# du earlier on GpSimd, its transposes and copies one slot earlier, delta replicated with 16 transfers

## The chip, the cores and the metric

The program runs on one core of a Trainium2 chip. The metric is the device time of one execution in microseconds, the median of several runs. A core has five engines that run their own instruction streams and meet only at semaphores: TensorE (PE in the profile, its weight loads PEld), VectorE (DVE), ScalarE (ACT), GpSimd (POOL) and the SyncE queue (SP), which here only issues DMA transfers.

## The reference

A Mamba network of four layers over 16 sequences of 256 tokens with 128 features, then a layer norm, a mixture of experts (8 experts, the best 2 of each token) and a second layer norm, all in float32. The part that the change touches is one layer:

```python
xp, z = split(rmsnorm(x) @ Win)
xc = silu(conv4(xp) + conv_b)
dt, B, C = split(xc @ Wx)
delta = softplus(dt @ Wdt + bdt)
for t in range(T):            # per channel d (256) and state n (16)
    h = exp(delta[t] * A) * h + (delta[t] * xc[t]) * B[t]
    y[t] = sum_n(h * C[t])
x = x + ((y + xc * D) * silu(z)) @ Wblk
```

`delta * xc` is called du in the kernel, exp(delta*A) decay, du*B dbu.

## The kernel before

Tokens go in 8 groups of 512 (two sequences), layers in 4, so there are 32 steps (`STEPS`). A step has 16 slots (`SLOTS`): slot 4m+p scans for state block m (0 to 3) and the pair p of channel units 2p and 2p+1. A unit is 32 channels times 4 states on the 128 partitions. For every slot VectorE runs one scan (L799) over 1024 columns and, for even slots, the product by C (L808, issued after the next scan). GpSimd makes the product by C of the odd slots (`times_c`, L466). TensorE adds the products up over the states (`quad`, L1000) into y.

What a scan needs is made by three engines. ScalarE makes decay with two exponentials per slot (`exps`, L545) from `d_rep`, in which delta stands four times, once for each group of 32 partitions. `outer` makes dbu with time on the partitions, from the transposed du (`du_t`) and a column of B: for each m there are 16 products, eight on GpSimd (L457 and L460) and eight on ScalarE (L623). TensorE turns them back (`to_channels`, L1015, eight transposes per slot) into `dbu_ps`, which has two buffers, so the transposes of slot n wait for scan n-2. Only at the first pair of each m do they also wait for all 16 products.

The order on each engine is written out by hand, as code under `if slot == ...` in five functions named `window(s, i, par)`. The window of step s holds the scans of step s and everything that prepares step s+1: convolution and projections, softplus (ScalarE at slots 7 and 8, VectorE after scan 8, where L838 gives `delta_ready`), du on GpSimd (L484), du's eight transposes on TensorE (`turn_du`, L1093), their two copies on ScalarE (`copy_dut`, L608), and the products of m = 0. The `SHARE`, `FIRST`, `POOL_SHARE` and `POOL_FIRST` tuples at the top say how many of the products are issued at which slot. The steps are unrolled but for the middle ones, which are a loop over pairs of windows (`par` 0 and 1).

`replicate` (L351) issues the copies of delta into `d_rep`: for each of 8 units and 4 partition groups one transfer of 32 partitions by 512 elements, 64 KB. Four semaphores per buffer (`rep_ready`) count them, one for each pair p; the exponentials of m = 0 wait for their pair's.

## Time and profile before

| | |
|---|---|
| median of 3 runs | 2284.54 us (2284.45 to 2295.04) |
| profiled execution | 2288.18 us, its span 2286.4 us |
| mean granted TensorE clock | 0.923 |
| busy in the span | VectorE 1951.5 us (85%), TensorE 1921.3 (84%), ScalarE 1687.4 (74%), GpSimd 1508.2 (66%) |
| first scan, last scan start | 67.0 us, 1823.6 us |

The span is from the first to the last instruction. About 1755 us of it is the 32 steps, the rest is the start and the experts at the end. A time in a timeline row is counted from the start of the span, so the same instruction can be compared across engines; a bracket at a row's end gives how long the engine stood idle before the row, and what it waited for. A busy share is a mean over stages and says nothing of which wait ended last.

### The profile page before, as it was taken

To read this page: it belongs to the slowest core of one execution; us is meant where nothing else is said; L and a number is where in the kernel's file an instruction comes from. 1 tells how busy PE (TensorE), PEld (TensorE's weight loads), DVE (VectorE), ACT (ScalarE), POOL (GpSimd) and SP (SyncE) were. 2 spreads that over 40 slices of the span, in tenths; PEclk is the share of its full clock that TensorE was granted. 3 is DMA by queue.
4 is the path that set the end of the run, shared out by engine and by line. 5 is a ranking of instruction groups with operands and counts; after the bars stand their busy time and mean duration, and the time that the engine had idled before them with its cause. 6 is when DMAs were issued, how large, how long until landed. Compare 5 with 4: busy or idle time off the path is not lost.

```text
span 2286.4 us, 35098 instructions
## 1 busy us (share of the span) xinstructions
PE 1921.3 (84%) x10784; PEld 1205.6 (53%) x10784; DVE 1951.5 (85%) x1824; ACT 1687.4 (74%) x3050; POOL 1508.2 (66%) x1365
## 2 busy tenths in 40 slices
PE   4688888888888888888888788888887689999998
PEld 1444444444444444444444444444444368998998
DVE  3799898998999998998999999998999976776776
ACT  3888888888888888888888888888888423333333
POOL 2688888888888888888888888888888700000000
PEclk8899998999999999999999999998999889999999
DMA  7323222222222323232323223222322200000000
GB/s 233 80 66 74 66 73 58 73 58 73 58 73 58 74 59 75 60 76 59 75 61 77 75 66 76 65 76 60 76 62 66 92 1 10 10 11 10 9 6 10
DMA packets 81482, 139.49 MB, mean 61 GB/s; under 512 B 21264, under 2 KB 39312, under 8 KB 76816
## 3 DMA queue, kind: packets, MB, share of 16 engines
q1 hardware_dynamic: 75024, 120.36, 20.5%
q10 hardware_dynamic: 6400, 18.42, 3.3%
q8 instruction: 30, 0.49, 0.1%
q14 instruction: 28, 0.23, 0.0%
HBM read 63.85 MB, written 7.74 MB: 31 GB/s over the span
## 4 chain that ended last, share of the span: by engine, by line
PE 34%; ACT 23%; POOL 17%; issue 11%; DVE 7%; ACTq 1%; POOLq 0%; DVEq 0%
PE y_ps L1215 10%; ACT decay L545 9%; POOL scan L466 8%; PE dbu_ps L1191 8%; POOL scan L460 8%; PE dbu_ps L1015 6%; PE pre_ps L1028 5%; ACT scan L623 5%; DVE scan L799 5%; PE pre_ps L1038 2%; POOL scan L457 2%; ACT sp_e L582 1%; ACT delta L583 1%; PE y_ps L1000 1%; ACT sp_l L592 1%
## 5 line engine op out<-in xcount | busy, mean ns | idle before, releaser
L799 DVE TENSOR_TENSOR_SCAN scan<-decay,dbu_ps 128x1024 f32<-128x1024 f32 x512 | 1157.3, 2276 | 151.4 <-PE dbu_ps L1015 147.1
L466 POOL TENSOR_TENSOR scan<-scan,c_rep 128x1024 f32<-128x1024 f32 x256 | 722.8, 2823 | 263.3 <-DVE scan L799 190.0
L1015 PE MATMUL dbu_ps<-ident,scan 128*128 128x128 f32 x4096 | 605.3, 296 | 287.3 <-DVE scan L799 181.9
L1015 PEld LDWEIGHTS dbu_ps<-ident,scan 128*128 128x128 f32 x4096 | 505.3, 152 | 619.7 <-DVE scan L799 303.8
L545 ACT ACTIVATE decay<-d_rep,a_cur 128x510 f32<-128x510 f32 x1024 | 670.7, 710 | 138.3 <-DMA d_rep<-delta 82.5
L460 POOL TENSOR_SCALAR scan<-du_t,b_t 128x256 f32<-128x256 f32 x896 | 591.5, 677 | 0.0
L623 ACT ACTIVATE scan<-du_t,b_t 128x256 f32<-128x256 f32 x1024 | 442.5, 494 | 1.2
L808 DVE TENSOR_TENSOR scan<-scan,c_rep 128x1024 f32<-128x1024 f32 x256 | 328.0, 1281 | 0.0
L1000 PE MATMUL y_ps<-scan,sel 128*32 128x512 f32 x2048 | 300.5, 661 | 5.7 <-POOL scan L466 5.7
L737 ACT ACTIVATE decay<-dbu_ps 128x512 f32<-128x512 f32 x256 | 148.6, 598 | 209.8 <-PE dbu_ps L1191 198.7
L1028 PE MATMUL pre_ps<-xn,w_pre 128*128 128x512 f32 x512 | 274.5, 663 | 5.7 <-DVE w_pre L788 4.9
L495 POOL TENSOR_TENSOR sp_e<-sp_e,bout_rep 128x512 f32<-128x512 f32 x8 | 10.9, 1361 | 295.9 <-DMA sp_e<-in_x_rows 295.9
L955 DVE TENSOR_TENSOR decay<-decay 128x512 f32<-128x512 f32 x256 | 164.5, 687 | 22.9 <-ACT decay L737 21.8
L1191 PE MATMUL dbu_ps<-y_parts,w_hi 128*128 128x512 f32 x512 | 166.3, 406 | 6.3 <-issue 5.6
L1028 PEld LDWEIGHTS pre_ps<-xn,w_pre 128*128 128x128 f32 x512 | 100.0, 217 | 110.9 <-issue 104.4
L942 DVE SCALAR_TENSOR_TENSOR xc<-y_ps,cw,xc 128x128 f32<-128x128 f32 x256 | 72.1, 344 | 100.5 <-PE y_ps L1215 100.5
L1215 PEld LDWEIGHTS y_ps<-w_pre,decay 128*128 128x128 f32 x1024 | 120.7, 194 | 5.5 <-issue 3.0
L1215 PE MATMUL y_ps<-w_pre,decay 128*128 128x128 f32 x1024 | 121.2, 277 | 2.5 <-DVE decay L955 2.5
L1215 PEld LDWEIGHTS y_ps<-c_rep,decay 128*128 128x128 f32 x1024 | 118.5, 192 | 2.0
L1215 PE MATMUL y_ps<-c_rep,decay 128*128 128x128 f32 x1024 | 118.5, 275 | 0.0
L1191 PEld LDWEIGHTS dbu_ps<-y_parts,w_hi 128*128 128x128 f32 x512 | 93.8, 192 | 24.7 <-issue 6.1
L1191 PE MATMUL dbu_ps<-y_parts,w_lo 128*128 128x512 f32 x256 | 101.5, 397 | 0.0
(105 smaller groups left out, 1737.7 us busy)
## 6 DMA issues: line engine op xcount, KB each, us to landing
d_rep<-delta SPq DMA_DIRECT2D x1024, 64.0 KB, 2.0
c_rep<-c_rows SPq DMA_DIRECT2D x32, 1024.0 KB
w_pre<-prepared_weights ACTq DMA_DIRECT2D x15, 866.0 KB, 10.4
prepared_weights<-scan SPq DMA_DIRECT2D x3, 1122.0 KB, 23.9
scan<-in_conv_w SPq DMA_DIRECT2D x4, 512.0 KB, 4.6
w_out<-prepared_weights SPq DMA_DIRECT2D x16, 128.0 KB, 9.8
sp_e<-in_x_rows SPq DMA_DIRECT2D x8, 256.0 KB, 3.3
d_rep<-in_w ACTq DMA_DIRECT2D x2, 1024.0 KB, 7.5
```

Of the source, the lines that this page charges most:

```text
L460: nc.gpsimd.tensor_scalar(dst, src, col, 1.0, ALU.mult, ALU.mult).then_inc(dbut_pool, 1)
L466: nc.gpsimd.tensor_tensor(ring[slot % RING], ring[slot % RING], c_rep[par][:, slot // PRS, :].unsqueeze(1).broadcast_to([128, 2, TG]), ALU ...
L545: last = nc.scalar.activation(decay[slot % DEC][:, u, :, 1:], src[:, :, 1:], ACT.Exp, scale=a_cur[:, b, m:m + 1])
L623: nc.scalar.activation(dbu_t[m % 2][:, j, :, q, :], du_t[par][:, j, :].rearrange("p (b c) -> p b c", b=UNITS), ACT.Copy, scale=b_t[par][:, ...
L799: nc.vector.tensor_tensor_scan(ring[slot % RING].rearrange("p u t -> p (u t)"), decay[slot % DEC].rearrange("p u a t -> p (u a t)"), dbu_p ...
L808: nc.vector.tensor_tensor(ring[slot % RING], ring[slot % RING], c_rep[par][:, slot // PRS, :].unsqueeze(1).broadcast_to([128, 2, TG]), ALU ...
L955: nc.vector.tensor_tensor(hid[e % 2][:, c, :], hid[e % 2][:, c, :], hid[e % 2][:, c, :], ALU.mult).then_inc(h2_ready, 1)
L1000: last = nc.tensor.matmul(y_ps[k][CH * j:CH * j + CH, :], sel[:, :], ring[slot % RING][:, j % 2, :], start=False, stop=m == M - 1, skip_gr ...
L1015: last = nc.tensor.transpose(dbu_ps[slot % 2][:, u, 128 * j:128 * j + 128], dbu_t[m % 2][:, j, b, :, :].rearrange("p q c -> p (q c)"), ide ...
L1028: tap = nc.tensor.matmul(o, w_pre[:, c0:c0 + 128], xn[:, :, k:k + SEQ], start=k == 0, stop=k == KC - 1, skip_group_check=True)
L1191: last = nc.tensor.matmul(dst, left[l], right[r], start=start and n == 0, stop=stop and n == len(passes) - 1)
L1215: last = nc.tensor.matmul(moe_ps[e % 2][:, DM * j:DM * j + DM], hid[e % 2][:, c, 128 * j:128 * j + 128], w2_sb[e][:, c, :], start=c == 0, ...
```

## The change

The diff makes four edits:

1. GpSimd issues du at the start of slot 10, before the last two products of m = 3 and the product by C of slot 9 that stand in that slot. It was behind them.
2. TensorE issues du's transposes at the end of slot 11, not of slot 12. ScalarE's copy of the previous group's output out of the same PSUM bank (`copy_out`, L630), which the transposes wait for, goes from slot 12 to slot 11.
3. ScalarE issues du's two copies at slot 14, not 15, and its eight products of m = 0 as 3, 3 and 2 at slots 14, 15 and 0, where it had 3 and 5 at slots 15 and 0.
4. `replicate` issues 16 transfers of 128 KB: one brings row group r of both halves k, that is units r and r+4. Two semaphores count them. Pairs 0 and 2 wait for the first eight transfers, pairs 1 and 3 for the last eight.

`POOL_FIRST` becomes (0, 0, 2, 3, 4): GpSimd's products of m = 0 are dealt out otherwise over slots 13 and 14, between which no other GpSimd instruction stands.

```diff
--- before.py
+++ after.py
@@ -46,9 +46,9 @@
 POOL_OUTER = Q * POOL_J
 ACT_OUTER = Q * (JT - POOL_J)
 SHARE = (0, 2, 5, 8)
-FIRST = (0, 3, 8)
+FIRST = (0, 3, 6, 8)
 POOL_SHARE = (0, 2, 3, 4, 4)
-POOL_FIRST = (0, 0, 1, 3, 4)
+POOL_FIRST = (0, 0, 2, 3, 4)
 
 
 W_CONV = 0
@@ -224,7 +224,7 @@
         dbut_pool = sem("dbut_pool")
         dbut_act = sem("dbut_act")
         dbu_ready = sem("dbu_ready")
-        rep_ready = [[sem(f"rep_ready{i}_{p}") for p in range(PRS)] for i in range(2)]
+        rep_ready = [[sem(f"rep_ready{i}_{p}") for p in range(2)] for i in range(2)]
         a_cur_ready = sem("a_cur_ready")
         decay_ready = sem("decay_ready")
         scan_done = sem("scan_done")
@@ -345,11 +345,11 @@
 
                 wait(sp, decay_ready, SLOTS * (s - 1))
                 sp.wait_ge(delta_ready, s + 1)
-                for b in range(UNITS):
-                    k, row = b // Q, CH * (b % Q)
+                by_row = d_rep[par].rearrange("p (k r) t -> p r k t", k=KT)
+                for r in range(Q):
                     for q in range(Q):
-                        sp.dma_start(d_rep[par][CH * q:CH * q + CH, b, :], delta[row:row + CH, k, :])\
-                            .then_inc(rep_ready[par][b // 2], 16)
+                        sp.dma_start(by_row[CH * q:CH * q + CH, r, :, :], delta[CH * r:CH * r + CH, :, :])\
+                            .then_inc(rep_ready[par][r // 2], 16)
 
             def load_input(g, n, par):
 
@@ -471,6 +471,10 @@
                 nxt = 1 - par
                 for slot in range(SLOTS):
                     m = slot // PRS + 1
+                    if slot == 10 and has(s, 1):
+                        pool.wait_ge(delta_ready, s + 2)
+                        nc.gpsimd.tensor_tensor(du[:, :, :], delta[:, :, :], xc[nxt][:, :, :], ALU.mult)\
+                            .then_inc(du_ready, 1)
                     if m < M and has(s, 0):
                         outer(s, par, m, POOL_SHARE[slot % PRS], POOL_SHARE[slot % PRS + 1])
                     if m == M and has(s, 1):
@@ -479,10 +483,6 @@
                         times_c(s - 1, i if par else i - 1, nxt, SLOTS - 1)
                     elif slot % 2 == 0 and slot and has(s, 0):
                         times_c(s, i, par, slot - 1)
-                    if slot == 10 and has(s, 1):
-                        pool.wait_ge(delta_ready, s + 2)
-                        nc.gpsimd.tensor_tensor(du[:, :, :], delta[:, :, :], xc[nxt][:, :, :], ALU.mult)\
-                            .then_inc(du_ready, 1)
                     if slot == 7 and has(s, 2):
                         normalise(s + 2)
                     if slot == 4 and is_last(s):
@@ -537,7 +537,7 @@
             def exps(s, i, par, slot):
                 m, p = slot // PRS, slot % PRS
                 if m == 0:
-                    act.wait_ge(rep_ready[par][p], 2 * Q * 16 * (i + 1))
+                    act.wait_ge(rep_ready[par][p % 2], 2 * Q * 16 * (i + 1))
                 wait(act, scan_done, SLOTS * s + slot - DEC + 1)
                 for u in range(2):
                     b = 2 * p + u
@@ -656,7 +656,7 @@
                         exps(s, i, par, slot)
                     m, p = slot // PRS + 1, slot % PRS
                     if has(s, 0) and slot == 0:
-                        outer(s, par, 0, FIRST[1], FIRST[2])
+                        outer(s, par, 0, FIRST[2], FIRST[3])
                     if has(s, 0) and m < M and p:
                         outer(s, par, m, SHARE[p - 1], SHARE[p])
                     if slot == 0 and has(s, 2):
@@ -678,14 +678,15 @@
                             load_w_pre(i)
                     if slot == 10 and has(s, 1):
                         copy_bt(s + 1, nxt)
-                    if slot == 12 and has(s, -1):
+                    if slot == 11 and has(s, -1):
                         copy_out(s - 1)
                     if slot == 12 and par == 1 and has(s, 0) and has(s, 1):
                         act.wait_ge(skip_done, s + 1)
                         load_w_skip(i)
-                    if slot == 15 and has(s, 1):
+                    if slot == 14 and has(s, 1):
                         copy_dut(s + 1, nxt)
-                        outer(s + 1, nxt, 0, FIRST[0], FIRST[1])
+                    if slot >= 14 and has(s, 1):
+                        outer(s + 1, nxt, 0, FIRST[slot - 14], FIRST[slot - 13])
                     if is_last(s):
                         if slot == 4:
                             copy_x(0)
@@ -1132,7 +1133,7 @@
                         turn_b(s + 1)
                     if slot == 9 and has(s, -1):
                         project_out(s - 1, i if par else i - 1, nxt)
-                    if slot == 12 and has(s, 1):
+                    if slot == 11 and has(s, 1):
                         turn_du(s + 1)
                     if slot >= 14 and has(s, 2):
                         if par == 0:
```

GpSimd, slots 8 to 13 of one window, as a difference (`-` before, `+` the change). L466 is the product by C, L457 and L460 the products that make dbu, L484 and L476 du:

```order
 L466 TENSOR_TENSOR scan<-scan,c_rep 128x1024 [waits scan_done]
-L460 TENSOR_SCALAR scan<-du_t,b_t 128x8x32 x4
+L460 TENSOR_SCALAR scan<-du_t,b_t 128x8x32 x2
+L476 TENSOR_TENSOR sp_l<-delta,xc 128x1024 [waits delta_ready]
+L460 TENSOR_SCALAR scan<-du_t,b_t 128x8x32 x2
 L466 TENSOR_TENSOR scan<-scan,c_rep 128x1024 [waits scan_done]
-L484 TENSOR_TENSOR sp_l<-delta,xc 128x1024 [waits delta_ready]
 L466 TENSOR_TENSOR scan<-scan,c_rep 128x1024 [waits bt_ready,scan_done,dut_ready,dbu_ready]
 L457 TENSOR_TENSOR scan<-du_t,b_t 128x8x32 [waits bt_ready,dut_ready,dbu_ready]
```

du moved ahead of two products of m = 3 and of the product by C of slot 9; the next product by C (slot 11) stands behind the wait for du's copies (`dut_ready`) as it did.

TensorE, slots 11 to 13, before. L1015 are `to_channels`, L1000 a `quad`, L1093 du's transposes:

```order
L1015 MATMUL dbu_ps<-ident,scan 128x128 [waits scan_done]
L1015 MATMUL dbu_ps<-ident,scan 128x128 x7
L1000 MATMUL y_ps<-scan,sel 32x512 [waits hc_pool,hc_dve]
L1000 MATMUL y_ps<-scan,sel 32x512 x3
L1015 MATMUL dbu_ps<-ident,scan 128x128 [waits scan_done,dbut_act,dbut_pool]
L1015 MATMUL dbu_ps<-ident,scan 128x128 x7
L1093 MATMUL pre_ps<-ident,sp_l 128x128 [waits x_ready,bt_ready,du_ready]
L1093 MATMUL pre_ps<-ident,sp_l 128x128 x7
```

and the same place in the change, where every line number is one higher:

```order
L1016 MATMUL dbu_ps<-ident,scan 128x128 [waits scan_done]
L1016 MATMUL dbu_ps<-ident,scan 128x128 x7
L1001 MATMUL y_ps<-scan,sel 32x512 [waits hc_pool,hc_dve]
L1001 MATMUL y_ps<-scan,sel 32x512 x3
L1094 MATMUL pre_ps<-ident,sp_l 128x128 [waits x_ready,bt_ready,du_ready]
L1094 MATMUL pre_ps<-ident,sp_l 128x128 x7
L1016 MATMUL dbu_ps<-ident,scan 128x128 [waits scan_done,dbut_act,dbut_pool]
L1016 MATMUL dbu_ps<-ident,scan 128x128 x7
```

du's transposes moved ahead of the eight transposes for scan 12.

ScalarE, from slot 14 of one window to slot 0 of the next, as a difference. L545 are exponentials, L608 du's copies, L623 products of m = 0:

```order
-L545 ACTIVATE decay<-d_rep,a_cur 128x2x255 [waits scan_done]
-L545 ACTIVATE decay<-d_rep,a_cur 128x2x255
 L608 ACTIVATE du_t<-pre_ps 128x512 [waits dut_mm] x2
 L623 ACTIVATE scan<-du_t,b_t 128x8x32 [waits bt_ready,dut_ready,dbu_ready]
 L623 ACTIVATE scan<-du_t,b_t 128x8x32 x2
+L545 ACTIVATE decay<-d_rep,a_cur 128x2x255 [waits scan_done]
+L545 ACTIVATE decay<-d_rep,a_cur 128x2x255
+L623 ACTIVATE scan<-du_t,b_t 128x8x32 x3
 L545 ACTIVATE decay<-d_rep,a_cur 128x2x255 [waits scan_done,rep_ready1_0]
 L545 ACTIVATE decay<-d_rep,a_cur 128x2x255
-L623 ACTIVATE scan<-du_t,b_t 128x8x32 x5
+L623 ACTIVATE scan<-du_t,b_t 128x8x32 x2
```

The copies and the first three products passed the exponentials of slot 15, and three of the five products left for slot 0 did too.

## Rows read from the trace of the kernel before

**Rows 1.** The waits of VectorE from 112 to 1735 us: total, times, longest.

```profile
DVE scan L799 <- PE dbu_ps L1015: 116.0, 90, 2.6
```

**Rows 2.** Busy time by engine in one step, from its first scan to the next's.

```profile
949.34:1005.34 56.00, 47.23 (x245) 25.74 (x244) 50.16 (x29) 47.67 (x87) 47.50 (x44) 0.90 0.32 75
```

**Rows 3.** VectorE's timeline: start, duration, instruction, idle before it and its releaser.

```profile
984.66 1.19 DVE L808 TENSOR_TENSOR scan<-scan,c_rep 128x1024 f32<-128x1024 f32 x1
990.16 1.33 DVE L808 TENSOR_TENSOR scan<-scan,c_rep 128x1024 f32<-128x1024 f32 x1
...
1001.50 1.26 DVE L808 TENSOR_TENSOR scan<-scan,c_rep 128x1024 f32<-128x1024 f32 x1
1005.34 2.29 DVE L799 TENSOR_TENSOR_SCAN scan<-decay,dbu_ps 128x1024 f32<-128x1024 f32 x1 [2.58 <-PE dbu_ps L1015]
1008.57 2.29 DVE L799 TENSOR_TENSOR_SCAN scan<-decay,dbu_ps 128x1024 f32<-128x1024 f32 x1 [0.94 <-PE dbu_ps L1015]
1012.39 2.29 DVE L799 TENSOR_TENSOR_SCAN scan<-decay,dbu_ps 128x1024 f32<-128x1024 f32 x1 [0.42 <-PE dbu_ps L1015]
```

**Rows 4.** TensorE's timeline in the same step.

```profile
986.70 1.93 PE L1000 MATMUL y_ps<-scan,sel 128*32 128x512 f32 x8
988.56 1.52 PE L1015 MATMUL dbu_ps<-ident,scan 128*128 128x128 f32 x8
990.53 1.09 PE L1093 MATMUL pre_ps<-ident,sp_l 128*128 128x128 f32 x8 [0.45 <-POOL sp_l L484]
...
998.35 1.99 PE L1028 MATMUL pre_ps<-xn,w_pre 128*128 128x512 f32 x4
1003.24 1.96 PE L1015 MATMUL dbu_ps<-ident,scan 128*128 128x128 f32 x8 [2.91 <-POOL scan L460]
```

**Rows 5.** TensorE at another boundary between two steps.

```profile
283.92 1.09 PE L1015 MATMUL dbu_ps<-ident,scan 128*128 128x128 f32 x8 [2.91 <-POOL scan L460]
```

**Rows 6.** VectorE at that other boundary.

```profile
287.64 2.29 DVE L799 TENSOR_TENSOR_SCAN scan<-decay,dbu_ps 128x1024 f32<-128x1024 f32 x1 [0.20 <-PE dbu_ps L1015]
```

**Rows 7.** GpSimd's timeline in the step of rows 3 and 4.

```profile
978.13 4.76 POOL L460 TENSOR_SCALAR scan<-du_t,b_t 128x256 f32<-128x256 f32 x4
984.83 3.26 POOL L466 TENSOR_TENSOR scan<-scan,c_rep 128x1024 f32<-128x1024 f32 x1 [1.94 <-DVE scan L799]
988.04 2.36 POOL L484 TENSOR_TENSOR sp_l<-delta,xc 128x1024 f32<-128x1024 f32 x1
...
992.73 2.38 POOL L466 TENSOR_TENSOR scan<-scan,c_rep 128x1024 f32<-128x1024 f32 x1 [2.33 <-ACT du_t L608]
...
995.65 3.26 POOL L460 TENSOR_SCALAR scan<-du_t,b_t 128x256 f32<-128x256 f32 x5
...
1001.21 1.90 POOL L460 TENSOR_SCALAR scan<-du_t,b_t 128x256 f32<-128x256 f32 x2
```

**Rows 8.** ScalarE's timeline in that step, and once at the start of the program.

```profile
61.53 1.33 ACT L545 ACTIVATE decay<-d_rep,a_cur 128x510 f32<-128x510 f32 x2 [13.31 <-DMA d_rep<-delta]
...
987.74 3.86 ACT L545 ACTIVATE decay<-d_rep,a_cur 128x510 f32<-128x510 f32 x6
991.51 1.06 ACT L608 ACTIVATE du_t<-pre_ps 128x512 f32<-128x512 f32 x2
...
1004.59 1.33 ACT L545 ACTIVATE decay<-d_rep,a_cur 128x510 f32<-128x510 f32 x2 [2.46 <-DMA d_rep<-delta]
```

**Rows 9.** SyncE's transfers of delta in that step: start and time to issue all.

```profile
982.63 20.51 SPq L351 DMA_DIRECT2D d_rep<-delta  x32
```

**Rows 10.** The page's costliest groups, ScalarE's products: busy, mean ns, idle before.

```profile
L623 ACT ACTIVATE scan<-du_t,b_t 128x256 f32<-128x256 f32 x1024 | 442.5, 494 | 1.2
```

**Rows 11.** Issue of the output transfers (256 KB each): ns min/median/max.

```profile
L408 SPq DMA_DIRECT2D out<-delta x8: 377/389/400, 1913.8 to 2283.6; - x8
```

**Rows 12.** Busy by engine, clock, DMA share and GB/s in two stretches.

```profile
990.00:1003.10 13.10, 9.63 (x57) 5.15 (x56) 12.77 (x8) 12.11 (x25) 10.78 (x12) 1.00 0.44 105
...
1003.24:1005.20 1.96, 1.96 (x9) 1.96 (x10) 0.00 (x0) 0.61 (x1) 1.96 (x5) 0.50 0.25 59
```

## The prediction

> **What bounds the kernel now.** I read the waits of each engine first, from the second step to the 31st. VectorE is the engine that the steps run on: in one step of 56.00 us it is busy 50.16 us [rows 2], more than any other. Almost all that it lacks is one wait: scans for TensorE's transposes, 116.0 us in 90 waits [rows 1]. VectorE's timeline shows where they are: three per boundary between two steps, at scans 0, 1 and 2 (30 boundaries in that stretch), 2.58, 0.94 and 0.42 us in the step that I work with [rows 3], 116.0 / 30 = 3.87 us at a boundary in the mean. From there one goes back by the releasers. TensorE's transposes for scan 0 start at 1003.24, although TensorE was done with its work before at 998.35 + 1.99 = 1000.34; they waited for GpSimd's last product of m = 0 [rows 4], which ended at 1001.21 + 1.90 = 1003.11 [rows 7]. GpSimd had stood still for 2.33 us before 992.73, for ScalarE's copies of du [rows 7]. These came at 991.51 to 992.57, behind six exponentials [rows 8], and du's transposes had been done only at 991.62, having waited 0.45 us for du [rows 4], which GpSimd made at 988.04 to 990.40, 5.4 us after delta was ready: SyncE's copies of delta, which wait for the same semaphore, start at 982.63 [rows 7, 9]. So the chain is delta, du, transposes, copies, GpSimd's products, transposes, scan 0. The change shortens just this chain.
>
> **The chain, step by step**, in the times of that step.
>
> *du.* It starts at 982.6, like SyncE's copies, and takes 2.36 us [rows 7]: 985.0, 5.4 us earlier. Before it GpSimd has done two of the four products that begin at 978.13, by about 980.5, and then waits 2.1 us for delta with the other two queued behind it. Nobody misses them: they end at about 987, and their reader is the transpose block for scan 12, which began at 988.56 before [rows 4]. The product by C of slot 9 follows, 987 to 989.4; before it ended at 988.1. It is read by a `quad` at slot 13, after 991.
>
> *Transposes.* They follow the `quad` that ends at 986.70 + 1.93 = 988.63. Eight transposes took 1.52 us there [rows 4], so they end at 990.1, 1.5 us earlier. Now the block for scan 12 stands behind them, and ends at 990.1 + 1.1 = 991.2; VectorE wants it at 990.16 + 1.33 = 991.49 [rows 3]. That is a margin of 0.3 us. With both blocks at the slow length of 1.96 us [rows 4] it would be missed by 1.1 us. I charge 0.15 us.
>
> *Copies.* `copy_out` and the exponentials of slot 12 only change places, so ScalarE comes to slot 13 at 987.74 as before. The six exponentials from there are those of slots 13 to 15, 3.86 us [rows 8]; now only four stand ahead of the copies: 987.74 + 2.57 = 990.3. `copy_out` is done in front of them, in time for the transposes at 988.6. The copies, 1.06 us, end at 991.4, where they ended at 992.57: 1.1 us earlier. It is the exponentials that set them now, not the transposes (990.1). Behind the copies stand eight products of m = 0 at 0.49 [rows 10] and the exponentials of slots 15 and 0 at 1.3 a slot, to about 998; scan 15 wants its decay at 999, scan 0 at 1002.8.
>
> *GpSimd's products.* From 992.73 to 1003.11 GpSimd is busy without a gap, 10.38 us, so its end moves with its start, by 1.1 us. It gains something on top: the last two products take 1.90 us, against 0.65 us each in the five before them [rows 7], beside VectorE's product by C at 1001.50 [rows 3]; when they are over before that begins they take 0.9. End: 991.5 + 10.4 - 0.9 = 1001.0, bounds 1000.5 to 1002.0.
>
> *Scan 0 and scan 1.* TensorE, free at 1000.34, starts its block at 1001.2 after 0.8 us of idleness, not 2.9. The granted clock in this block was 0.50, half of full speed, that is the 1.2 GHz level, while it was 1.00 (2.4 GHz) in the 13 us before [rows 12], and the block took 1.96 us. At another boundary, after the same idleness, it took 1.09 us [rows 5]. With 0.8 us of idleness I take the short one: 1002.3. VectorE comes free at 1001.50 + 1.26 = 1002.76. The wait of 2.58 us is gone. At the boundary with the short block scan 1 waited only 0.20 us [rows 6], with VectorE starting as early as TensorE allowed; now it starts 0.4 us later than that, so this wait is gone too. What is late next is TensorE's row of blocks before scan 2: of the 0.42 us I leave 0.3. Scans 3 to 15 keep their distances.
>
> *The 16 transfers.* 32 issues take 20.51 us, 0.64 each, until 1003.14 [rows 9]. ScalarE waited for the last one until 1004.59, at the exponentials of slot 3 [rows 8], so it lands 1.5 to 2 us after its issue. In the shortened step that would be too late, so the edit matters. The trace has no transfer of this form (32 partitions by 2 by 512). If the price is per issue, 16 take 10.3 us, and all has landed at 995. If it is per byte, 20.5 us. The nearest rows: an output transfer of four times the size, cut in the same way along the free axis, has an issue of 0.39 us [rows 11], and while these copies run alone the DMA engines are busy 0.44 at 105 GB/s [rows 12], so twice the rate would be 0.88: they can just follow. I take 0.65 us each, end 995.1, perhaps 997 where weights are loaded beside it. The exponentials of slot 1 now need all 16 transfers, and come at about 998.
>
> *Start.* The first step waited 13.31 us for its first eight transfers behind stores of weights [rows 8]. Eight now carry twice the bytes: 512 KB more. Between -1 and +5 us, once; I take +2.
>
> **A rule weighed.** VectorE's product by C took 1.19 us at 984.66 and 1.33 us at 990.16, when du was in its last 0.24 us; GpSimd's product by C took 3.26 us when it began together with one of VectorE's and 2.38 otherwise [rows 3, 7]. So the two hold each other up. du now runs over 984.66 to 985.0, and VectorE's product there may be held up by 0.3 us; at 990.16 it no longer is. I charge 0.2 us of VectorE per step for this and for changed meetings elsewhere. The Trainium skill (SBUF — State Buffer, "Who interferes with whom") says that a VectorE instruction with two SBUF inputs and a GpSimd instruction that reads SBUF exclude each other, and that the later one is blocked until the other is through. Taken in full, a VectorE product that comes just after a GpSimd product by C began would lose all its 2.4 us, against the 0.14 us that is seen at 990.16.
>
> **Sum.** 3.87 - 0.3 (left at scan 2) - 0.15 (scan 12) - 0.2 (held up) - 0.17 (boundaries with the long block in one of six, 1 us each) = 3.05 us at a boundary. Times 31 boundaries: 94.5. Less 2 at the start: 92.5. From the profiled execution, 2288.18, that leaves 2195.7. The median of the runs is 3.64 us below it, so I predict 2192.
>
> **Rivals.**
>
> A, transfers priced by byte: slower than before. At 1.28 us each the last lands at 1005.1. Before, slot 1 needed only half of the transfers; now its exponentials stand until 1005.1, and behind them on ScalarE the rest of slots 1 to 3 (three pairs of exponentials and eight products, some 7.5 us), then `silus`, at 1012.6. Before, these followed the exponentials at 1004.59 and three products [rows 8, 10], at 1007.4. Of the 5.2 us ScalarE makes up a part, where it waits for TensorE after that: between 0 and 5.2 us are lost per step, and I take 2.3: 31 x 2.3 = +71, 2356. It decides from 16 transfers that take over 0.88 us each (loss of part of the gain) and 1.14 us each (loss of all). For it: an untried form, and the low DMA reserve. Against it: [rows 11, 12].
>
> B, half the gain: TensorE's block for scan 0 stays long. It ends at 1003.2, scan 0 waits 0.4 us, and scan 1 waits 0.9 as in [rows 3], scan 2 0.4. 3.87 - 1.7 - 0.35 = 1.8 per boundary: -56 + 2, 2231. For it: the long block is the usual one before. Against it: the idleness ahead of it goes from 2.9 to 0.8 us.
>
> C, GpSimd in VectorE's way. With m = 0 done at 1001.1 GpSimd goes straight into four products (2.4 us, and 0.9 held up at 1001.5) and its product by C of slot 15, about 1004.4 to 1006.8; VectorE's next product by C comes after scans 0 and 1, at 1002.8 + 4.5 = 1007.3. If GpSimd is 0.6 us later, VectorE comes while it runs and is held up by about 2 us: 3.05 - 2 = 1.05 per boundary, 2254. This is where the skill's rule would bring it in full.
>
> D, no gain: a wait on the chain that I did not see (du's transposes kept by something else) leaves the copies where they are: 2284.
>
> **Chances.** Forecast 0.65 (own range 2176 to 2214), B 0.14, C 0.08, D 0.05, A 0.08. A change under 0.5%, 11 us, is about what a measurement of this kernel can't tell from none. Faster: 0.65 + 0.14 + 0.08 = 0.87, same 0.05, slower 0.08. Range: from 2175 (3.6 us gained at each boundary) to 2256, which takes in B and C.
>
> **What would show it.** Right: the waits of scans for transposes fall from 116 us to 10 or 20, the step is about 52.1 us; du begins within 0.2 us of delta; copies about 1.1 us earlier in the step; TensorE's idleness before the block for scan 0 under 1 us and the block at 1.1 us; the 16 transfers issued in 10 to 11 us and no wait of ScalarE for `d_rep` but at the start. Wrong: transfers that take over 0.9 us each with ScalarE waiting at slot 1 (A); a long block at clock 0.5 (B); VectorE's products by C above 2 us (C); copies of du no earlier (D).

## The result, and the profile after

| | before | changed |
|---|---|---|
| median | 2284.49 us (2278.19 to 2295.04, 4 runs) | 2177.46 us (2173.84 to 2182.44, 4 runs) |
| ratio to before | | 0.9529, 95% interval 0.9487 to 0.957 |
| profiled execution, its span | 2288.18, 2286.4 us | 2175.6, 2173.8 us |
| mean granted TensorE clock | 0.923 | 0.942 |

The change makes the kernel 4.7% faster, 107 us between the medians and 112.6 us between the profiled executions. 2192 us was forecast, with 2175 to 2256 as the range: right, and 14.5 us too cautious. One execution of e1 (2778.65 us) and one of e7b (3671.61 us), both experiments further down, lie far outside all others of their kernels and are in no median or ratio here.

First VectorE's waits, from the second step to the 31st, in the changed kernel (total, times, longest):

```profile
DVE sp_w L831 <- ACT sp_l L592: 21.1, 29, 0.8
DVE scan L800 <- PE dbu_ps L1016: 7.4, 15, 1.1
DVE scan L800 <- ACT decay L545: 3.8, 11, 0.4
```

The scans waited 116.0 us in 90 waits for TensorE [rows 1] and now 7.4 us in 15. Nothing of that size has come in its place. One step of the changed kernel, from its first scan to the next's (length, then busy of TensorE, weight loads, VectorE, ScalarE, GpSimd, then clock, DMA share, GB/s):

```profile
945.46:997.09 51.63, 44.76 (x247) 24.15 (x246) 50.33 (x31) 48.58 (x89) 46.04 (x44) 0.97 0.28 64
```

VectorE does the same work, 50.33 us against 50.16, in 51.63 us in place of 56.00 [rows 2]. It is now busy 97% of the step. The chain itself, in the changed kernel's timelines of this step. VectorE makes delta, and then waits neither for scans 0 and 1 (997.09) nor for scan 2 (1002.74):

```profile
975.54 1.23 DVE L839 TENSOR_TENSOR delta<-delta,sp_l 128x1024 f32<-128x1024 f32 x1
...
995.76 1.41 DVE L809 TENSOR_TENSOR scan<-scan,c_rep 128x1024 f32<-128x1024 f32 x1
997.09 4.45 DVE L800 TENSOR_TENSOR_SCAN scan<-decay,dbu_ps 128x1024 f32<-128x1024 f32 x2
...
1002.74 2.29 DVE L800 TENSOR_TENSOR_SCAN scan<-decay,dbu_ps 128x1024 f32<-128x1024 f32 x1
```

SyncE's transfers and GpSimd's du, both right behind delta:

```profile
976.84 10.24 SPq L351 DMA_DIRECT2D d_rep<-delta  x16
```

```profile
976.85 2.35 POOL L476 TENSOR_TENSOR sp_l<-delta,xc 128x1024 f32<-128x1024 f32 x1 [2.42 <-DVE delta L839]
...
985.06 2.93 POOL L466 TENSOR_TENSOR scan<-scan,c_rep 128x1024 f32<-128x1024 f32 x1 [1.64 <-ACT du_t L608]
...
994.11 0.94 POOL L460 TENSOR_SCALAR scan<-du_t,b_t 128x256 f32<-128x256 f32 x2
```

TensorE, with du's transposes (L1094) and the block for scan 0 at 995.19:

```profile
982.59 1.09 PE L1094 MATMUL pre_ps<-ident,sp_l 128*128 128x128 f32 x8
...
995.19 1.09 PE L1016 MATMUL dbu_ps<-ident,scan 128*128 128x128 f32 x8 [0.56 <-POOL scan L460]
```

ScalarE, six exponentials and then du's two copies:

```profile
980.17 3.78 ACT L545 ACTIVATE decay<-d_rep,a_cur 128x510 f32<-128x510 f32 x6
983.84 1.06 ACT L608 ACTIVATE du_t<-pre_ps 128x512 f32<-128x512 f32 x2
```

delta ends at 976.77. du begins 0.08 us behind it, the copies end 8.1 us behind it, GpSimd's last product of m = 0 ends at 995.05, and TensorE's block comes after 0.56 us of idleness, not 2.91, and is short. It is over at 996.28, before VectorE is free.

The same reading for all 31 boundaries between two steps gives the table that the experiments are compared by. Its numbers are means made from the timelines, in us. A step is the mean of the 30 from the second step's scan 0 to the 32nd's; the next two columns count from the end of delta. A block (the eight transposes for scan 0) is called long when it takes over 1.5 us.

| kernel | step | copies begin, end | block for scan 0 begins | long blocks |
|---|---|---|---|---|
| before | 55.17 | 8.97, 10.04 | 20.71 | 21 of 31 |
| changed | 51.38 | 7.47, 8.59 | 18.52 | 0 of 31 |
| e1 | 54.99 | 8.96, 10.02 | 20.68 | 20 of 31 |
| e2 | 52.26 | 7.47, 8.58 | 18.53 | 0 of 31 |
| e3 | 55.69 | 9.17, 10.23 | 21.00 | 30 of 31 |
| e4 | 53.26 | 8.96, 10.21 | 20.17 | 1 of 31 |
| e5 | 55.53 | 9.17, 10.23 | 20.98 | 29 of 31 |
| e6 | 51.62 | 7.83, 8.92 | 18.79 | 1 of 31 |
| e8 | 54.61 | 8.76, 9.84 | 20.53 | 23 of 31 |

3.79 us per step, 31 times, is 117.5 us; the profiled executions differ by 112.6. The rest went the other way at the start. VectorE's first scan is at 69.1 and not 67.0, and scan 3 waits 3.87 us and not 1.48, so that the softplus of the second step stands 4.8 us later. What ScalarE waited for, and SyncE's transfers there, in the changed kernel:

```profile
41.57 21.98 SPq L351 DMA_DIRECT2D d_rep<-delta  x16
...
64.76 1.33 ACT L545 ACTIVATE decay<-d_rep,a_cur 128x510 f32<-128x510 f32 x2 [15.55 <-DMA d_rep<-delta]
```

13.31 us of waiting [rows 8] have become 15.55.

### The profile page after: what moved, and what is told of

It reads as the page before. It is cut to its first block, busy times and chain, and to the rows that moved or that the text cites. A ratio compares the mean times of both kernels' runs of the same rounds, so it can differ in the third digit from the quotient of the medians.

```text
span 2173.8 us, 34586 instructions
## 1 busy us (share of the span) xinstructions
PE 1875.8 (86%) x10784; PEld 1179.1 (54%) x10784; DVE 1943.6 (89%) x1824; ACT 1682.6 (77%) x3050; POOL 1460.3 (67%) x1365
## 4 chain that ended last, share of the span: by engine, by line
ACT 29%; POOL 26%; PE 25%; issue 12%; DVE 5%; SPq 1%; DMA 1%; ACTq 1%; POOLq 0%; DVEq 0%
POOL scan L466 12%; ACT decay L545 11%; POOL scan L460 11%; PE y_ps L1216 11%; PE dbu_ps L1192 8%; ACT scan L623 7%; DVE scan L800 3%; POOL scan L457 2%; ACT sp_e L582 2%; ACT delta L583 2%; ACT sp_l L592 2%; PE dbu_ps L1016 2%; ACT sp_e L587 1%; SPq L351 1%; ACT du_t L608 1%
## 5 line engine op out<-in xcount | busy, mean ns | idle before, releaser
L1016 PE MATMUL dbu_ps<-ident,scan 128*128 128x128 f32 x4096 | 570.4, 286 | 236.4 <-DVE scan L800 198.8
L466 POOL TENSOR_TENSOR scan<-scan,c_rep 128x1024 f32<-128x1024 f32 x256 | 676.3, 2642 | 140.8 <-DVE scan L800 75.8
L1016 PEld LDWEIGHTS dbu_ps<-ident,scan 128*128 128x128 f32 x4096 | 479.8, 146 | 516.6 <-DVE scan L800 266.6
L545 ACT ACTIVATE decay<-d_rep,a_cur 128x510 f32<-128x510 f32 x1024 | 668.1, 709 | 72.0 <-DMA d_rep<-delta 29.6
L460 POOL TENSOR_SCALAR scan<-du_t,b_t 128x256 f32<-128x256 f32 x896 | 592.7, 677 | 0.0
L623 ACT ACTIVATE scan<-du_t,b_t 128x256 f32<-128x256 f32 x1024 | 445.6, 494 | 1.2
L809 DVE TENSOR_TENSOR scan<-scan,c_rep 128x1024 f32<-128x1024 f32 x256 | 330.8, 1292 | 0.0
L1029 PE MATMUL pre_ps<-xn,w_pre 128*128 128x512 f32 x512 | 248.4, 608 | 5.6 <-DVE w_pre L789 4.8
L1029 PEld LDWEIGHTS pre_ps<-xn,w_pre 128*128 128x128 f32 x512 | 88.9, 193 | 99.1 <-issue 92.7
L476 POOL TENSOR_TENSOR sp_l<-delta,xc 128x1024 f32<-128x1024 f32 x32 | 75.2, 2350 | 83.7 <-DVE delta L839 83.7
## 6 DMA issues: line engine op xcount, KB each, us to landing
w_pre<-prepared_weights ACTq DMA_DIRECT2D x15, 866.0 KB, 13.8
```

The costliest lines, as they stand in the source:

```text
L460: nc.gpsimd.tensor_scalar(dst, src, col, 1.0, ALU.mult, ALU.mult).then_inc(dbut_pool, 1)
L466: nc.gpsimd.tensor_tensor(ring[slot % RING], ring[slot % RING], c_rep[par][:, slot // PRS, :].unsqueeze(1).broadcast_to([128, 2, TG]), ALU ...
L545: last = nc.scalar.activation(decay[slot % DEC][:, u, :, 1:], src[:, :, 1:], ACT.Exp, scale=a_cur[:, b, m:m + 1])
L623: nc.scalar.activation(dbu_t[m % 2][:, j, :, q, :], du_t[par][:, j, :].rearrange("p (b c) -> p b c", b=UNITS), ACT.Copy, scale=b_t[par][:, ...
L809: nc.vector.tensor_tensor(ring[slot % RING], ring[slot % RING], c_rep[par][:, slot // PRS, :].unsqueeze(1).broadcast_to([128, 2, TG]), ALU ...
L1016: last = nc.tensor.transpose(dbu_ps[slot % 2][:, u, 128 * j:128 * j + 128], dbu_t[m % 2][:, j, b, :, :].rearrange("p q c -> p (q c)"), ide ...
```

## The experiments

**The transfers by themselves.** e1 is the kernel before with edit 4 alone, e2 the changed kernel without it.

```diff
-                for b in range(UNITS):
-                    k, row = b // Q, CH * (b % Q)
+                by_row = d_rep[par].rearrange("p (k r) t -> p r k t", k=KT)
+                for r in range(Q):
                     for q in range(Q):
...
-                    act.wait_ge(rep_ready[par][p], 2 * Q * 16 * (i + 1))
+                    act.wait_ge(rep_ready[par][p % 2], 2 * Q * 16 * (i + 1))
```

e1:

> The kernel before with the 16 transfers alone. Theory (the transfers shorten nothing while the chain delta, du, transposes, copies, GpSimd's products sets the boundary): the waits of scans for transposes stay near 116 us from the second step to the 31st, the waits of ScalarE for d_rep go, and only the start costs something, +4.8 us as after: 2284.5 + 4.8 = 2289, between 2280 and 2292. Rival (ScalarE's waits for d_rep, 67 us in 35 waits, were on the path): about 2220 to 2250.

e2:

> The changed kernel with the 32 transfers of before. Theory: the last of them lands 22 us after delta, ScalarE comes to the exponentials of slot 3 at 19.3 us after delta, waits 2.7 us there, and the projection of z is 1.1 us late in each step (0.5 to 1.6): 2177.5 + 31 x 1.1 - 4.8 (the start as before) = 2207, between 2188 and 2225. Rival (the transfers are hidden in the changed kernel too): 2173, only the start is better. Second rival (all of the gain hangs on them): 2280.

e1: 2290.68 us, ratio 1.0019 (0.9993 to 1.0045), no change. e2: 2200.1 us, ratio 0.9627 (0.9579 to 0.9675), about 1% behind the changed kernel. ScalarE's wait for delta's transfers between 112 and 1735 us, first in the kernel before (there that is the second step to the 31st):

```profile
ACT decay L545 <- DMA d_rep<-delta: 67.1, 35, 2.5
```

then in e2:

```profile
ACT decay L545 <- DMA d_rep<-delta: 74.7, 37, 3.9
```

and VectorE's in e1 and in e2:

```profile
DVE scan L799 <- PE dbu_ps L1015: 111.5, 90, 2.6
```

```profile
DVE scan L800 <- PE dbu_ps L1016: 27.1, 60, 3.5
```

In e1 the 16 transfers cut ScalarE's 67 us of waiting to 14 us and VectorE waits nearly as before: those waits were hidden. In the shortened step the late last transfer is felt, as argued, at 0.88 us per step (52.26 and not 51.38). So edit 4 is worth nothing alone and about 1% beside the others.

**The copies.** e5 is the changed kernel with ScalarE's order of before (copies at slot 15, products 3 and 5). e8 is the reverse, the kernel before with that order alone changed.

```diff
-FIRST = (0, 3, 6, 8)
+FIRST = (0, 3, 8)
...
-                    if slot == 14 and has(s, 1):
-                        copy_dut(s + 1, nxt)
-                    if slot >= 14 and has(s, 1):
-                        outer(s + 1, nxt, 0, FIRST[slot - 14], FIRST[slot - 13])
+                    if slot == 15 and has(s, 1):
+                        copy_dut(s + 1, nxt)
+                        outer(s + 1, nxt, 0, FIRST[0], FIRST[1])
```

e5:

> The changed kernel with ScalarE's two copies of du at slot 15 again, behind all exponentials, and its products of m = 0 as 3 at slot 15 and 5 at slot 0; du and the transposes stay early, the transfers are 16. Theory (the place of the copies sets GpSimd's start): the copies end 10.0 us after delta as before, not 8.1, GpSimd's last product of m = 0 ends near 20.3 us after delta, the waits at scans 0 and 1 come back nearly whole: 2270 to 2289, say 2280. Rival (du and its transposes made the gain): under 2200.

e8:

> The kernel before with ScalarE's part alone: copies at slot 14, products of m = 0 as 3, 3 and 2. Theory: the copies stand ready at 7.7 us after delta but du's transposes end only 9.0 us after it, behind du; the copies end 9.7 us after delta, 0.3 us earlier than before: ratio 0.996, between 0.990 and 1.001. Rival (ScalarE's order was all that held the copies, du and transposes were early enough): 0.975 or less.

e5: 2303.79 us, ratio 1.0072 (1.0046 to 1.0097). The whole gain is gone, which was expected, and 0.7% more, which was not. e8: 2270.15 us, ratio 0.9913 (0.9886 to 0.994), where 0.996 (0.990 to 1.001) was expected. In e8 ScalarE comes to the copies earlier and waits there for du's transposes (ScalarE's waits, second step to 31st):

```profile
ACT du_t L608 <- PE pre_ps L1094: 39.3, 29, 1.8
```

So the copies' place is what releases the gain, 126 us between e5 and the changed kernel, and by itself it buys less than 1%, because du and with it the transposes are late: these end 9.08 us behind delta, as in the kernel before (9.09).

**du's place.** e3 is the kernel before with du moved ahead as in edit 1, e4 the changed kernel with du back behind the product by C of slot 9.

```diff
+                    if slot == 10 and has(s, 1):
+                        pool.wait_ge(delta_ready, s + 2)
+                        nc.gpsimd.tensor_tensor(du[:, :, :], delta[:, :, :], xc[nxt][:, :, :], ALU.mult)\
+                            .then_inc(du_ready, 1)
                     if m < M and has(s, 0):
                         outer(s, par, m, POOL_SHARE[slot % PRS], POOL_SHARE[slot % PRS + 1])
...
-                    if slot == 10 and has(s, 1):
-                        pool.wait_ge(delta_ready, s + 2)
-                        nc.gpsimd.tensor_tensor(du[:, :, :], delta[:, :, :], xc[nxt][:, :, :], ALU.mult)\
-                            .then_inc(du_ready, 1)
```

e3:

> The kernel before with du alone moved ahead of the last two products of m = 3 and the product by C of slot 9. Theory: du is 5.4 us earlier and its transposes, still at slot 12, 0.45 us, but the copies start where they did, since the exponentials of slot 15 stand before them; GpSimd's wait for du's copies grows by what du no longer fills. No gain: ratio 1.000, between 0.996 and 1.003. Rival (du is the first link and its 5.4 us count, at least the 0.45 us): 0.990 or less.

e4:

> The changed kernel with du behind the product by C of slot 9 again; transposes at slot 11, copies at slot 14, 16 transfers. Theory: TensorE reaches du's transposes 5.8 us after delta and waits for du until 7.9; the block for scan 12 stands behind them and ends 10.1 us after delta, 1.25 us after VectorE wants it. VectorE loses that in every step and the copies come 1.5 us later, which the boundary then takes up: 2177.5 + 31 x 1.25 = 2216, ratio 0.970, between 0.964 and 0.976, with a wait of about 1.2 us at scan 12. Rival (TensorE's slack covers it): 0.953.

e3: 2304.2 us, ratio 1.0056 (1.0031 to 1.0081), where no change was expected: a miss, of the same kind as e5's. e4: 2232.93 us, ratio 0.9741 (0.9714 to 0.9768); 1.88 us per step are lost, not the 1.25 expected.

e4's loss is a wait at another place than before. TensorE waits for du and then makes its transposes, and the block for scan 12 (L1016) stands behind them. (The second row merges that block and the next one.) TensorE and then VectorE in e4:

```profile
1019.55 1.97 PE L1094 MATMUL pre_ps<-ident,sp_l 128*128 128x128 f32 x8 [1.90 <-POOL sp_l L484]
1021.31 2.73 PE L1016 MATMUL dbu_ps<-ident,scan 128*128 128x128 f32 x16
```

```profile
1023.29 4.46 DVE L800 TENSOR_TENSOR_SCAN scan<-decay,dbu_ps 128x1024 f32<-128x1024 f32 x2 [2.79 <-PE dbu_ps L1016]
```

This is the wait at scan 12 for which the prediction charged 0.15 us: the moved transposes need the moved du, and without it VectorE waits 2.2 us there in the mean and up to 2.85 us. The expectation had taken du's eight transposes at 1.1 us. They took 1.97 here, at a granted clock of 0.50 (1.2 GHz) after 1.90 us of idleness, and over 1.9 us in 15 of 31 steps.

e3's and e5's loss shows in the timelines. VectorE's product by C behind scan 9 and scan 0 of the next step, in e3:

```profile
1048.60 1.40 DVE L808 TENSOR_TENSOR scan<-scan,c_rep 128x1024 f32<-128x1024 f32 x1
...
1069.62 2.29 DVE L799 TENSOR_TENSOR_SCAN scan<-decay,dbu_ps 128x1024 f32<-128x1024 f32 x1 [3.05 <-PE dbu_ps L1015]
```

ScalarE and TensorE in e3:

```profile
1054.41 1.33 ACT L545 ACTIVATE decay<-d_rep,a_cur 128x510 f32<-128x510 f32 x2 [0.74 <-DVE scan L799]
1055.65 1.06 ACT L608 ACTIVATE du_t<-pre_ps 128x512 f32<-128x512 f32 x2
```

```profile
1067.50 1.97 PE L1015 MATMUL dbu_ps<-ident,scan 128*128 128x128 f32 x8 [3.16 <-POOL scan L460]
```

du (1046.57 to 1048.92) runs into VectorE's product, which takes 1.40 us where it took 1.19 [rows 3]. The scans behind it come 0.2 us later; the exponentials of slot 15 wait for one of them (0.74 us), and the copies stand behind these exponentials: 9.17 and not 8.97 us after delta in the table. GpSimd ends 0.3 us later, TensorE's idleness grows from 2.91 to 3.16 us, and its block is long at 30 of 31 boundaries, not 21, though many of these take 1.5 to 1.7 us: in the mean it takes 1.83 us and not 1.73. Counted from delta, scan 0 comes 0.42 us later (0.30 for the start of the block, 0.11 for its length), scan 1 another 0.28 later, and the rest of the step is 0.16 shorter: 0.54 us a step, some 16 us in all, which is the difference of the profiled executions; the ratio of the medians makes 13. In e5 the same sum is 0.40 us a step, 12 us, and the late first transfers of the 16 (delta of the second step is ready at 105.1 and not 99.6) bring the other 5. The changed kernel has the same meeting of du and product, but there the copies don't stand behind that scan. No run took the meeting alone away, so this account is read from the timelines, and is not shown by a run.

**The transposes.** e6 is the changed kernel with du's transposes back at slot 12.

```diff
-                    if slot == 11 and has(s, 1):
+                    if slot == 12 and has(s, 1):
                         turn_du(s + 1)
```

> The changed kernel with du's transposes behind the block for scan 12 (slot 12) again. Theory: du is there long before, so they run 1.1 us later, the copies end 0.5 us later, and TensorE's block for scan 0, which is 0.8 us ahead of VectorE in the changed kernel, takes that up: 2177.5, within 5 us. Rival (the earlier transposes carry the 1.5 us): 31 x 1.1 = +34, 2211.

2182.18 us, ratio 0.9544 (0.9497 to 0.9591), which can't be told from the changed kernel. The copies begin 0.36 us later and the step is 0.24 us longer in the profiled execution. Early copies and early du carry the gain, and the move of the transposes next to nothing.

**The start.** Two theories of why the first transfers of delta land so late: they share the DMA engines with the stores of the prepared weights, or with the load of the C rows, which SyncE also issues before them. The second came up only with e7's result. e7 issues the stores ahead of that load.

```diff
+                if not has(s, 0) and has(s, 1):
+                    for l in range(1, LAYERS):
+                        sp.wait_ge(made_ready, l + 1)
+                        sp.dma_start(w_dram[l, :, :], made[:, l, :]).then_inc(made_stored[l], 16)
                 if has(s, 1):
                     sp.wait_ge(c_stored, 16 * (s + 2))
...
                     if not has(s, 0):
-                        for l in range(1, LAYERS):
-                            sp.wait_ge(made_ready, l + 1)
-                            sp.dma_start(w_dram[l, :, :], made[:, l, :]).then_inc(made_stored[l], 16)
```

> The changed kernel with one more edit at the program's start: SyncE issues the stores of the prepared weights of layers 1 to 3 as soon as they are made, 20 to 26 us, ahead of its wait for the first rows of C, not after it at 31.9. Theory (the first transfers of delta stand behind 3.4 MB of stores in the same queue, ScalarE waits 15.5 us for them and VectorE's first scan starts at 69.1): the stores are through some 10 us earlier, the first scan starts at 56 to 60, 2177.5 - 11 = 2166, ratio 0.948, between 0.945 and 0.952, and nothing after the first step changes. Rival (the transfers of delta are slow in themselves at the start, or the stores collide with the loads before): the first scan stays later than 65 and the ratio at 0.953.

2171.49 us, ratio 0.9479 (0.9458 to 0.9499). The first scan was expected at 56 to 60 and is at 68.4, a miss: ScalarE still waits for the transfers. The load of C rows, now behind the stores, is issued at 36.26 and not 31.17:

```profile
36.26 0.66 SPq L375 DMA_DIRECT2D c_rep<-c_rows  x1
```

```profile
64.11 1.33 ACT L546 ACTIVATE decay<-d_rep,a_cur 128x510 f32<-128x510 f32 x2 [13.75 <-DMA d_rep<-delta]
```

So the stores are not it, or not they alone. The load is one transfer of 1 MB: it reads four rows of 8 KB and writes each to 32 partitions. This is how the DMA engines look while one of these loads runs in the middle of the changed kernel, where little else moves:

```profile
1012.50:1016.00 3.50, 3.50 (x18) 1.90 (x15) 3.50 (x3) 3.47 (x7) 2.48 (x2) 1.00 0.21 47
1016.00:1020.00 4.00, 3.64 (x29) 2.21 (x28) 3.93 (x3) 4.00 (x9) 4.00 (x6) 1.00 0.24 57
1020.00:1025.00 5.00, 5.00 (x29) 2.52 (x28) 4.28 (x3) 4.26 (x6) 5.00 (x4) 1.00 0.25 62
```

A steady share of 0.21 to 0.25 is about what 4 of 16 engines would give. e10 issues the load as four transfers, one for each partition group; e9 does that and e7's edit. The changed kernel itself (r1) and e7's (e7b) ran on the same chip beside them.

```diff
-                    sp.dma_start(merged(c_rep[nxt]),
-                                 bass.AP(tensor=rows.tensor, offset=rows.offset,
-                                         ap=[[M * TG, Q], [0, CH], [1, M * TG]]))\
-                        .then_inc(c_loaded[nxt], 16)
+                    for q in range(Q):
+                        sp.dma_start(merged(c_rep[nxt][CH * q:CH * q + CH, :, :]),
+                                     bass.AP(tensor=rows.tensor, offset=rows.offset + q * M * TG,
+                                             ap=[[0, CH], [1, M * TG]]))\
+                            .then_inc(c_loaded[nxt], 16)
...
-                    pool.wait_ge(c_loaded[par], 16 * (i + 1))
+                    pool.wait_ge(c_loaded[par], Q * 16 * (i + 1))
```

VectorE's wait for the same load changes in the same way.

e10:

> The changed kernel with the load of the C rows as four transfers of 32 partitions in place of one of 128. Theory: each of the four runs on all DMA engines, the megabyte passes in 5 us, not 17, and in the first step the transfers of delta no longer stand behind it: first scan at 58 to 62 instead of 69, steps unchanged at 51.4: 2177.5 - 9 = 2168. Rival (stores of 3.4 MB fill all engines anyway): first scan at 67 or later, no gain.

e9:

> Both: stores ahead of the wait for C, and the C rows in four transfers. Theory: nothing large is ahead of delta's transfers at 42.7, the first eight land near 50, first scan at 54 to 57: 2177.5 - 13 = 2164.5, the fastest of all. Rival: as for e10, first scan at 65 or later.

r1:

> The changed kernel itself, on the chip of the three runs that follow, as their measure. All theories: ratio to the kernel before 0.953, first scan at 69 us, step 51.4 us.

e7b:

> The kernel of e7 again, beside the changed one. Theory now (the first transfers of delta stand behind the load of the C rows, which moves 1 MB at 57 to 62 GB/s with the DMA engines busy 0.21 to 0.25, as if on four of sixteen, and which e7 issues 5 us later than the changed kernel does): first scan at 68 to 69 and no gain, -1 us, ratio 0.999 to 1.001 of the changed one. Rival (e7's median, 6 us below that of the changed kernel in other runs, was its own): -6 us.

| | median | ratio (95%) | first scan |
|---|---|---|---|
| r1 | 2177.91 | 0.9516 (0.9491 to 0.9541) | 69.2 |
| e7b | 2173.1 | 0.9501 (0.9475 to 0.9528) | 70.1 |
| e10 | 2159.93 | 0.9446 (0.9421 to 0.9471) | 55.4 |
| e9 | 2158.79 | 0.9441 (0.9417 to 0.9466) | 53.7 |

SyncE, ScalarE and a stretch of the middle with such a load in it, in e10:

```profile
32.20 1.73 SPq L372 DMA_DIRECT2D c_rep<-c_rows  x4
...
42.59 10.37 SPq L351 DMA_DIRECT2D d_rep<-delta  x16
```

```profile
52.01 1.33 ACT L546 ACTIVATE decay<-d_rep,a_cur 128x510 f32<-128x510 f32 x2 [1.78 <-DMA d_rep<-delta]
```

```profile
998.00:1003.00 5.00, 5.00 (x29) 2.49 (x28) 5.00 (x5) 4.67 (x9) 3.98 (x6) 1.00 0.57 139
```

The share is 0.57 in place of 0.25, ScalarE's wait falls from 15.55 to 1.78 us, the first scan comes 14 us earlier, and 18.0 us are gained over r1, twice the 9 us expected; e9 was expected to bring 13 and brought 19. Issuing the 16 transfers takes 10.37 us and not 21.98. It was the load of C rows, in the form of one transfer. Part of what came on top of the start is in the steps, 51.28 us and not 51.38 (r1): after the first step ScalarE never waits for `d_rep` in e10, where it waited 13.8 us in r1. The stores' place adds 1.1 us at most (e9 against e10), which these runs can't tell from nothing; e7b against r1 can't either (4.8 us between the medians, with overlapping intervals). e10 and e9 are faster than both kernels of this case.

## Why the prediction was right

The mechanism of the steps was the one given; that of the start was not, as the end of this section says. One by one:

- *du* begins 0.08 us behind delta, as predicted.
- *Transposes.* They end 7.49 us behind delta in the mean; 990.1 was 7.5 behind it.
- *Copies.* Foreseen 1.1 us earlier, and set by the exponentials. In the mean they end at 8.59 and not 10.04, 1.45 us earlier. That the exponentials set them, and not the transposes, is to be seen in ScalarE's wait for the transposes from the second step to the 31st, in the changed kernel and then in e6, where they come 0.5 us later and do begin to hold the copies up:

```profile
ACT du_t L608 <- PE pre_ps L1094: 1.2, 7, 0.2
```

```profile
ACT du_t L608 <- PE pre_ps L1094: 9.3, 15, 1.7
```

- *GpSimd's products, TensorE's block.* The block was to start 18.6 us behind delta (1001.2) and starts at 18.52. Idleness before it was to be 0.8 us and is 0.56 here. Over the steps TensorE's wait for GpSimd is 19.3 us in 30, against 87.1 in 30.
- *The 16 transfers* are priced per issue: 10.24 us, 0.64 each, against the 10.3 taken from [rows 9, 11]. Rival A, 1.28 us each, is out, and e1 shows that in the step of before they neither help nor harm. But "no wait of ScalarE for `d_rep` but at the start" did not come true: from the second step to the 31st there are 12 such waits, 12.9 us. The longest:

```profile
1043.69 1.33 ACT L545 ACTIVATE decay<-d_rep,a_cur 128x510 f32<-128x510 f32 x2 [3.03 <-DMA d_rep<-delta]
```

  This one and one of 2.97 us lengthen their steps to 53.13 and 53.41 us, where their neighbours take 51.0 to 51.7. All but the shortest stand in steps in which a load of 866 KB of weights is issued 3.8 us ahead of the transfers, beside the load of C rows. In e10, with the same weights and the C rows in four transfers, none is left. The prediction thought of the weights ("perhaps 997") and not of the C rows.
- Rival B (long block) is out with no long block at 31 boundaries, rival D with the copies' 1.45 us. Rival C is out too: GpSimd's products by C are shorter, not longer (2642 ns in the mean, before 2823), and VectorE's take 1292 ns against 1281. The meeting that it feared never came about: in neither kernel does a product of VectorE begin with more than 0.1 us of a GpSimd product by C still to run, so what such a meeting would cost is not shown here.

What was off is sizes. The steps' gain was put at 3.05 us and is 3.79. The terms of the sum, against what they measured:

| term per boundary | predicted | measured |
|---|---|---|
| left at scan 2 | 0.30 | 0.42 in 12 of 30, 0.17 in the mean |
| wait at scan 3 | not foreseen | 1.12 and 0.96, in the two long steps: 0.07 in the mean |
| wait at scan 12 | 0.15 | 0.2 once, 0.01 in the mean |
| VectorE held up by GpSimd | 0.20 | 0.09 ((330.8 - 328.0) / 31) |
| long blocks | 0.17 | none in 31 |

The four terms were 0.82 us together, and with the wait at scan 3 they came to 0.34: 0.48 us per step too cautious, 15 us in all. The rest of the gain, 3.79 + 0.34 - 3.87 = 0.26 us per step, is more than the wait on which the sum was built. Most of it is VectorE's own busy time, which I had let grow. Over the second to the 31st step (length, TensorE, weight loads, VectorE, ScalarE, GpSimd, clock, DMA share, GB/s) before:

```profile
112.00:1735.00 1623.00, 1363.39 (x7171) 740.52 (x7170) 1479.63 (x853) 1393.32 (x2510) 1377.77 (x1243) 0.92 0.27 68
```

and in the changed kernel:

```profile
112.00:1640.00 1528.00, 1332.85 (x7277) 726.12 (x7275) 1490.66 (x864) 1405.09 (x2538) 1345.73 (x1253) 0.94 0.31 72
```

That is 1479.63 us in 1623 / 55.17 = 29.4 steps, 50.3 a step, and 1490.66 in 1528 / 51.38 = 29.7, 50.1 a step. The products by C cost 0.09 us more. The largest part of what went the other way is the instruction that makes delta (ns min/median/max), before and in the changed kernel:

```profile
L838 DVE TENSOR_TENSOR delta<-delta,sp_l x32: 1224/1382/1383, 40.5 to 1751.9; 128x1024 f32<-128x1024 f32 x32
```

```profile
L839 DVE TENSOR_TENSOR delta<-delta,sp_l x32: 1224/1225/1381, 40.3 to 1644.2; 128x1024 f32<-128x1024 f32 x32
```

Before, GpSimd had four products to do while VectorE made delta (978.13 to 982.89 in [rows 7], delta from 981.16 to 982.54). Now two of them stand behind du, GpSimd is done early and idles for the 2.42 us shown above, and the instruction takes 0.16 us less. It takes 1382 ns in all kernels with du late (before, e1, e4, e8) and 1225 in all with du early (changed, e2, e3, e5, e6). The prediction saw GpSimd's idleness there and did not ask what it would spare VectorE.

The term on the other side, the start, was put at 2 us (-1 to +5) and is 4.8. So the profiled execution, forecast at 2195.7, took 2175.6, 20 us less. That the median is only 14.5 us off is in part luck: the profiled execution before lay 3.64 us above its median, which the forecast took off, and the changed one lies 1.9 us below its own. The sum had it right that the first transfers cost something and not why: the transfers of delta stood behind the load of C rows, where I read stores of weights; e7 moved the stores for nothing, and e10 shows the load.

The second thing the prediction did not see is how the parts depend on each other. It treats each edit as a piece of the chain with its own microseconds. Measured alone, du's early place costs 0.56%, the copies' place gives 0.9%, the transfers nothing; together they give 4.7%. What carries the gain is du and the copies moved both: e6, with the transposes left where they were, keeps nearly all of it, while e3 loses 0.56%, e8 gains 0.9%, and e4, with all but the early du, gains 2.6%.

## What to carry to other kernels

Follow the wait that ends last back through each engine and move all links of it together; a link moved alone can be worth nothing, or cost, because the next link was set by something else. An edit that removes waits that nothing else stands behind (the 16 transfers) has to be judged in the step that the other edits make, not in the old one. When a transfer lands late, look at the DMA share while its neighbours run: a share that stands at a quarter may point to a transfer whose shape uses few engines, and cutting it in pieces to see is cheap.

## What the runs showed of the hardware

- **A load that runs as if on a quarter of the DMA engines.** The C rows' load of 1 MB ran at a share of 0.21 to 0.25 and 47 to 62 GB/s; cut in four it ran at 0.57 and 139 GB/s, and the kernel gained 18.0 us. The source's outermost dimension is 4 in the one form and 32 in the other. The Trainium skill (DMA: Bandwidth & Descriptors, "Why a DMA increments its semaphore by 16 and not by 1") says that the number of engines is the largest one up to 16 that divides the outermost dimensions of both sides, which would be 4 here, and 16 for each of the four parts. The share of 0.21 to 0.25 agrees with 4; the 0.57 of the other form shows that more than 4 were at work (0.57 of 16 is 9), and not that it was 16.
- **Price of an issue.** 64 KB or 128 KB, 32 partitions each: 591 and 599 ns in the median. While the 16 large ones ran (976.80 to 987.00) the DMA engines were busy 0.89 at 198 GB/s, twice the 0.44 and 105 of [rows 12]. From issue to landing the median went from 2.0 to 3.1 us. There is little left for larger pieces.
- **TensorE's clock after idleness.** Eight transposes took 1.96 us at a granted clock of 0.50 (1.2 GHz) after 2.91 us of idleness [rows 4, 12], and at another boundary 1.09 us after the same [rows 5]. Before, they were long at 21 of 31 boundaries, with 2.8 to 2.9 us of idleness ahead of nearly all; in e3, with 3.0 to 3.2 us, at 30 of 31. In the changed kernel all 31 were short, 30 of them after less than 1 us and the last after 2.79. So the idleness just before does not decide it by itself: 2.79, 2.91 and 2.91 us gave both lengths.
- **VectorE and GpSimd.** Who begins first matters. Before, GpSimd's product by C began inside one of VectorE's 133 times: VectorE's then took 1.20 us in 130 of these, its usual time, and GpSimd's 3.25 us in the median, where it otherwise takes 2.36. When VectorE's product began while GpSimd was in the end of du it took 1.33 us before and 1.40 in the changed kernel. 0.2 us is small, and yet in e3 and e5 it seems to stand ahead of the chain.
